# Next image's group mean and variance one 3x3 tile later, and the last values projection behind the shift's row

## What is computed

```python
t = cbs(x, cv1_w, cv1_bn, 0)                 # 1x1 conv, batch norm, silu, on _gn(x)
ys = [t[:, :C], t[:, C:]]                    # C = 256
for i in range(N):                           # N = 2 blocks
    yi = ys[-1]
    z = cbs(yi, m_cv1_w[i], m_cv1_bn[i], 1)  # 3x3 conv
    z = bot_attention(z, m_qkv_w[i], m_rw[i], m_rh[i])   # softmax(q (k + r) / 8) v, 4 heads of 64
    z = jax.nn.silu(bn_eval(conv2d(z, m_cv2_w[i], 0), m_cv2_bn[i]))
    ys.append(yi + z)
x = x + cbs(jnp.concatenate(ys, axis=1), cv2_w, cv2_bn, 0)
...
def _gn(v, G=32, eps=1e-5):                  # v is (B_, C_, H_, W_)
    g = v.reshape(B_, G, C_ // G, H_, W_)
    m = jnp.mean(g, axis=(2, 3, 4), keepdims=True)
    s = jnp.var(g, axis=(2, 3, 4), keepdims=True)
    return ((g - m) / jnp.sqrt(s + eps)).reshape(v.shape)
```

## Time and profile before

| | us |
|---|---|
| median of 3 runs | 3354.56 (3351.9 to 3355.57) |
| the profiled execution | 3349.9 |
| its span, first to last instruction | 3347.9 |
| TensorE busy | 3072.6 |
| VectorE busy | 1871.9 |
| ScalarE busy | 1568.1 |
| GpSimd busy | 1047.1 |
| mean granted TensorE clock | 0.984 of full |
| from one image to the next (image 2 to 3) | 392.5 |

### The profile page before, as it was taken

The page is one execution under the profiler, slowest core; times in us unless marked ns, Lnnn a source line. Parts: engine busy times, 40 slices in busy tenths (PEclk is TensorE's granted clock), DMA queues, the critical chain, the costliest instruction groups (busy, mean ns, idle before and its releaser), DMA issues.

```text
span 3347.9 us, 61223 instructions
## 1 busy us (share of the span) xinstructions
PE 3072.6 (92%) x27308; PEld 1574.6 (47%) x27308; DVE 1871.9 (56%) x2515; ACT 1568.1 (47%) x1826; POOL 1047.1 (31%) x768
## 2 busy tenths in 40 slices
PE   3769999999998999999999999989999899999997
PEld 3524554454544545445444545435454454445453
DVE  5536465375654656455653657546564657537464
ACT  1315465173732746245651737327362455517382
POOL 1113451052511443134411525105431244115051
PEclk8889999999999999999999999999999999999998
DMA  4200000100011000100001000110001000000001
GB/s 144 73 26 30 1 30 26 64 17 29 11 51 44 2 29 23 54 29 2 30 26 51 30 29 8 38 60 2 29 20 57 29 1 30 26 26 30 1 8 44
DMA packets 35894, 105.60 MB, mean 32 GB/s; under 512 B 12976, under 2 KB 15024, under 8 KB 32944
## 3 DMA queue, kind: packets, MB, share of 16 engines
q1 hardware_dynamic: 35632, 101.69, 8.5%
HBM read 80.18 MB, written 21.50 MB: 30 GB/s over the span
## 4 chain that ended last, share of the span: by engine, by line
PE 76%; DVE 11%; ACT 6%; issue 4%; POOL 3%; SPq 0%; DMA 0%; POOLq 0%; DVEq 0%
PE ps_u L679 48%; PE ps_u L838 12%; DVE row_max L1199 4%; PE ps_o L860 4%; PE ps_o L861 3%; PE ps_o L862 3%; ACT wide L986 3%; PE ps_u L812 3%; PE ps_u L698 2%; DVE stats L1133 1%; POOL y_pad L1307 1%; ACT ps_u L986 1%; DVE qk L1188 1%; POOL z L1307 1%; PE ps_u L870 1%
## 5 line engine op out<-in xcount | busy, mean ns | idle before, releaser
L679 PE MATMUL ps_u<-y_pad,w_c 128*128 128x512 f16 x3456 | 792.7, 387 | 0.0
L1199 DVE TENSOR_REDUCE row_max<-ps_u 128x2 f32<-128x1024 f32 x512 | 617.5, 1220 | 189.7 <-PE ps_u L812 189.7
L1333 POOL TENSOR_TENSOR probs<-wide,probs 128x1024 f16<-128x1024 f32 x256 | 544.9, 2128 | 515.5 <-ACT probs L990 504.8
L1007 DVE SCALAR_TENSOR_TENSOR wide<-wide 128x512 f32<-128x512 f32 x256 | 182.5, 715 | 655.1 <-ACT wide L906 653.3
L679 PEld LDWEIGHTS ps_u<-y_pad,w_c 128*128 128x128 f16 x3456 | 333.0, 98 | 424.9 <-issue 28.0
L905 ACT ACTIVATE wide<-ps_u,par_m_t 128x512 f32<-128x512 f32 x128 | 99.3, 776 | 863.7 <-PE ps_u L679 863.7
L838 PE MATMUL ps_u<-qk 64*128 64x512 f16 x3072 | 418.7, 378 | 41.4 <-ACT shift_rows L978 19.6
L860 PEld LDWEIGHTS ps_o<-v_ext,probs 128*128 128x128 f16 x4096 | 375.9, 96 | 143.4 <-issue 128.9
L860 PE MATMUL ps_o<-v_ext,probs 128*128 128x65 f16 x4096 | 431.4, 193 | 0.0
L861 PE MATMUL ps_o<-v_ext,probs 128*128 128x64 f16 x4096 | 429.1, 195 | 0.0
L862 PE MATMUL ps_o<-v_ext,probs 128*128 128x65 f16 x4096 | 426.5, 192 | 0.0
(11 more groups left out here) (182 smaller groups left out, 3933.4 us busy)
## 6 DMA issues: line engine op xcount, KB each, us to landing
w_c<-w_c_dram SPq DMA_DIRECT2D x15, 2304.0 KB, 8.9
xn<-in_x_dram SPq DMA_DIRECT2D x32, 512.0 KB, 5.7
o_nat<-in_x_dram SPq DMA_DIRECT2D x64, 256.0 KB, 2.6
out_dram<-qk SPq DMA_DIRECT2D x32, 512.0 KB, 2.7
w_c_dram<-w_c SPq DMA_DIRECT2D x2, 2304.0 KB, 8.0
qk<-in_L_conv_m_cv_w_dram SPq DMA_DIRECT2D x2, 1152.0 KB, 7.1
probs<-in_L_conv_m_cv_w_dram SPq DMA_DIRECT2D x2, 1152.0 KB, 10.8
probs<-in_L_conv_cv_w_dram SPq DMA_DIRECT2D x2, 1024.0 KB, 12.0
```

Of the source, the lines that this page charges most:

```text
L679: ins = e.matmul(o, lhsT, rhs, start=start and k == 0, stop=stop and k == len(pairs) - 1)
L1199: e.reduce_max(row_max[:, g % 2, :, it, half], ps_u[:, use.slot:use.slot + 2, :], axis=AX.X).then_inc(*dve_max.up(i, b, g, half, it))
L1333: e.tensor_tensor(p_part(s, 1), wide[:, w.slot, :], p_part(s, 0), ALU.subtract).then_inc(*pool_lo.up("p", i, b, s))
```

## The change

Two edits of the order; no instruction is added or removed. `NORM_PARTS` for block 0 gives the parts behind the four tiles (0, 0), (1, 0), (0, 1), (1, 1) as 1, 0, 1, 1 where it gave 1, 1, 1, 0. So in images 0 to 6 `gn_mean` comes behind the third tile and `gn_var` behind the fourth. In all 16 blocks q(0,1) takes the place of v(3) between the maxima, and v(3) comes behind the shift's row. The order behind k(1,1) was: max, max, v(3), max, shift, max, q(0,1), shift's row, max. It is: max, max, q(0,1), max, shift, max, shift's row, v(3), max.

```diff
--- before.py
+++ after.py
@@ -392,9 +392,9 @@
         STEPS = len(GROUPS_OF) * JT
         MAX_AHEAD = 2
         LAST_MAX = STEPS - JT - MAX_AHEAD
-        NORM_PARTS = {(0, 0, 0): 1, (0, 0, 1): 1, (0, 1, 0): 1, (0, 1, 1): 0, (1, 0, 0): 2, (1, 0, 1): 1, (1, 1, 0): 1, (1, 1, 1): 0}
+        NORM_PARTS = {(0, 0, 0): 1, (0, 0, 1): 0, (0, 1, 0): 1, (0, 1, 1): 1, (1, 0, 0): 2, (1, 0, 1): 1, (1, 1, 0): 1, (1, 1, 1): 0}
         HALF_0 = (("q", 1, 0), ("k", 1, 0), ("v", 0), ("v", 1))
-        HALF_1 = ((("k", 0, 1), 0), (("v", 2), 1), (("k", 1, 1), 2), (("v", 3), 1), (("q", 0, 1), 0))
+        HALF_1 = ((("k", 0, 1), 0), (("v", 2), 1), (("k", 1, 1), 2), (("q", 0, 1), 2))
 
         def way(s):
 
@@ -461,9 +461,8 @@
                 piece(*at)
                 for _ in range(count):
                     next(maxima)
-                if at == ("v", 3):
-                    next(maxima)
             plan_shift_row(i, b, 0)
+            piece("v", 3)
             next(maxima)
 
             o_uses, threads = {}, []
```

## The result

| | before | after |
|---|---|---|
| median | 3354.28 us (3351.9 to 3356.98, 8 runs) | 3344.97 us (3342.26 to 3347.84, 8 runs) |
| span of the profiled execution | 3347.9 us | 3340.9 us |
| mean granted TensorE clock | 0.984 | 0.979 |

The ratio is 0.9974, 95% interval 0.9965 to 0.9984: the changed kernel is 9.3 us faster. The forecast was 23.5 us faster, 3331 us, with a range that ended at 3344. The sign is right and about 14 us are missing. The mean clock has fallen although one long wait is gone, which is the first hint.

A forecast was written before the change was run, and what follows sets the result against it. TensorE was taken to bound the kernel, with 76% of the chain that ended last. -47.7 + 24.2 = -23.5 us, from 3354.6 to 3331 us, range 3313 to 3344.

The forecast's parts named there:

- Part 1: First blocks of images 0 to 6: mean behind third tile, variance behind fourth, saves 6.81 us an image, 47.7 us.
- The variance at no cost: Variance behind the fourth tile: its 1.7 us on VectorE is covered by the splits' waits for ScalarE, put at 0.
- Part 2: All 16 blocks: q(0,1) ahead, v(3) behind the shift's row, makes first logits 1.51 us later, +24.2 us.
- That alone costs nothing: TensorE's idle time of about 1.6 us before the shift's row costs 0, since the shift sets the row's start.
- The third rival: Clock falls in the new stretch of each block: 1.9 us at most, 16 times, 30 us, giving 3361; chance 0.04.

The follow-up runs named there:

- e8: The kernel before, with 22 extra matmuls filling TensorE's wait in front of each of the seven group means: 3342.11 us, ratio 0.9967.
- e7: The kernel before, with mean and variance both moved behind the third tile and the old order of the values: 3354.12 us, ratio 1.0004.
- e5: e4 with the first logits given the bank pair of the row and v(3), and filled as e3: 3333.26 us, ratio 0.9943.
- e3: The changed kernel, with six extra matmuls a block while TensorE waits for the shift of group 0: 3330.67 us, ratio 0.9935.
- Part 1 alone: The kernel before with only the NORM_PARTS edit: 3304.41 us, ratio 0.9857.
- e4: The changed kernel, with one maximum moved ahead of v(3), behind the shift's row: 3339.48 us, ratio 0.9961.
- e2: The kernel before with only the reorder of q(0,1) and v(3): 3398.31 us, ratio 1.0137.

## Why the prediction was right and where it was wrong

- **Part 1, 6.81 us an image:** right. Measured 21.27 - 14.33 - 0.14 = 6.80 in image 2, and 47.4 us for the kernel alone against 47.7. Taking the price from image 7, where the step is missing, carried the slow clock with it (e8: 10.9 us of it); the wait alone would have given 34.6.
- **The variance at no cost:** right, 24.89 against 24.75 us with its own 0.14 us matmul in it. e7 shows what its new place is worth: next to the mean it gives all of Part 1 back.
- **Part 2, 1.51 us a block:** right as the cost of the waits, 1.52 in each of the 4 blocks in which the clock holds. e5 confirms the link that it rests on: the logits start with v(3)'s split.
- **"That alone costs nothing", said of TensorE's idle time before the shift's row:** this is the step that failed. The idle time delayed no step by itself, but it came with a fall of the granted clock to 0.50 in 12 of 16 blocks, 13.3 us, a term that the sum had at nothing. Filled with matmuls that nobody needs (e3), it costs 1.9 us, in two blocks, and the ratio is 0.9935, with the forecast's 0.9930 within the interval. In e3 an image takes 1417.19 - 1028.44 = 388.75 us (first q projections of images 2 and 3), where the forecast was 388.7; in the changed kernel it is 1424.58 - 1033.66 = 390.92.
- **The third rival** was this mechanism, with 4 in 100. I argued from the stretch of before, which has TensorE busy 7.05 of 10 us and keeps 1.00. The new stretch has it busy 2.24 of 4.88 us. Of eight stretches of 4.9 us that I have since read in the same block before, from 1067 to 1086, the sparsest has it busy 3.21 us:

```profile
1079.00:1083.90 4.90, 3.21 (x20) 1.12 (x22) 3.31 (x4) 3.81 (x4) 2.63 (x2) 1.00 0.00 0
```

Between the setup and the closing work of the last image, only the unbroken wait was sparser than the new stretch, and behind it the clock did fall. So the trace did not exclude the rival; I took a denser case for the case in question. Nor is the denser case safe by itself: here 3.21 of 4.90 us kept the clock, and in two blocks of e3 it fell behind 3.2 of 4.90. The rival's size, 1.9 us in all 16 blocks, was the upper end: measured are 0.7 to 1.9 in 12.
- The Trainium skill, "TensorE: Matmul & The Clock Gate", section "A second HAM failure mode: psum-queue depth-cycling", says that frequent short idles between groups of matmuls can make the clock go back and forth. The trace agrees: 12 stretches at 0.50 behind such idles, none with a single idle time above 1.6 us. The Trainium skill has them from cycling through PSUM banks; here the longest of them was a wait for VectorE's shift.

Part 2 is a loss by itself, and Part 1 alone beats both kernels: ratio 0.9857, some 39 us below the two together. What stays open is why a given block keeps its clock: images 2 and 3 show equal work before the row and different clocks behind it. It was not tried to shift the blocks in time to see whether that moves the falls.

## What to carry to other kernels

When a wait is removed or made, price the granted clock behind it too, and find that price where a twin of the stretch lacks the wait. Idle time of TensorE that moves no dependent step is not free by that alone: here it cost 13.3 us by the clock. Filling it with spare matmuls tells in one run whether the clock is what is lost. And in an order written by a planner, work the bank choice through again for each variant: a step moved by one place took away the wait of the first logits for v(3)'s split.

## What the runs showed of the hardware that was not expected

Adding work made two kernels faster: six matmuls a block, some 13 us (e3 against the changed kernel, by the ratios), and 22 an image, 10.9 us (e8 against before). With the same instructions the clock fell behind TensorE's 2.24 of 4.88 us in image 2 and not behind 2.26 of 4.90 in image 3. It fell behind 3.22 of 4.90 us in e3 and not behind 3.21 of 4.90 before. The spread from run to run doesn't tell where the clock falls: e4 spreads over 11.9 us, but e2, in which it falls in every block, over 2.7, and the kernel before, in which it falls in no block's attention, over 5.1.
